# Attention's extra products at other steps, small products behind the scores, statistics ahead of the maximum

## The reference, cut to what matters

```python
def _L1_attn_ref(x, w_qkv, w_out, b_out):
    ...
    dots = jnp.einsum('bhid,bhjd->bhij', q, k) * SCALE
    m = jax.nn.softmax(dots, axis=-1)
    diag = jnp.diagonal(m, axis1=-2, axis2=-1)
    mu = diag.mean(axis=-1, keepdims=True)
    sd = diag.std(axis=-1, ddof=1, keepdims=True)
    keep = jnp.abs((diag - mu) / sd) <= Z_THRESH
    valid = keep[..., :, None] & keep[..., None, :]
    masked = jnp.where(valid, dots, NEG)
    attn = jax.nn.softmax(masked, axis=-1)
    ...
    out = jnp.einsum('bhij,bhjd->bhid', attn, v)
    out = out.transpose(0, 2, 1, 3).reshape(b, n, h * d)
    return out @ w_out.T + b_out
```

## Time and profile before

| | |
|---|---|
| median of 3 runs | 1979.87 us (1979.25 to 1979.98) |
| the profiled execution's own time | 1980.71 us |
| its span, first to last instruction | 1979.4 us |
| TensorE busy | 1786.4 us (90%) |
| VectorE, ScalarE, GpSimd busy | 1404.6, 1159.7, 1193.8 us |
| granted TensorE clock, mean | 0.987 |
| attention, first `scores` to last head's end | about 736 to 1850 us |

### The profile page before, as it was taken

How to read it: one execution, slowest core, us unless ns; L and a number is a source line. 1 busy time by engine, 2 the same in 40 slices (tenths; PEclk the granted TensorE clock), 3 DMA queues, 4 the chain that set the end, 5 groups by cost and what they waited for, 6 DMA issues and landing times. The chain is left out here.

```text
span 1979.4 us, 29905 instructions
## 1 busy us (share of the span) xinstructions
PE 1786.4 (90%) x11064; PEld 1213.2 (61%) x11064; DVE 1404.6 (71%) x2493; ACT 1159.7 (59%) x1715; POOL 1193.8 (60%) x660
## 2 busy tenths in 40 slices
PE   9998999789998986899989899898989898988888
PEld 5873444336875654666666667666666676665466
DVE  5617899986427754677777777777777777787676
ACT  5326777745326456666666666666666666663544
POOL 5542767963535430576666767676767666667454
PEclk9998999999999997999999999999999999999999
DMA  2000000000000013212122121212121212100100
GB/s 96 1 0 0 0 0 0 0 1 0 1 20 29 1 51 75 52 45 58 45 48 55 38 64 35 68 35 58 45 57 46 57 45 56 44 12 17 53 6 16
DMA packets 43665, 66.03 MB, mean 33 GB/s; under 512 B 24769, under 2 KB 26177, under 8 KB 43265
## 3 DMA queue, kind: packets, MB, share of 16 engines
q1 hardware_dynamic: 43056, 63.54, 12.4%
q10 hardware_dynamic: 432, 0.59, 0.1%
q0 software_dynamic: 32, 0.00, 0.0%
HBM read 29.05 MB, written 1.24 MB: 15 GB/s over the span
## 5 line engine op out<-in xcount | busy, mean ns | idle before, releaser
L2409 POOL TENSOR_TENSOR at_e_lo<-at_e,at_e_hi 128x1024 fp32r<-128x1024 f32 x256 | 613.1, 2395 | 353.9 <-DVE at_e_hi L2382 348.4
L2165 ACT ACTIVATE at_e<-at_ps,at_dropped 128x1024 f32<-128x1024 f32 x256 | 285.7, 1116 | 199.7 <-PE at_ps L1878 189.3
L2157 ACT ACTIVATE at_ps<-at_ps,at_neg_diag 128x1024 f32<-128x1024 f32 x256 | 278.6, 1089 | 138.3 <-DVE at_neg_diag L2253 137.0
L2262 DVE CUSTOM_DVE_ANT_0 at_ps<-at_ps,at_mask 128x1024 f32<-128x1024 f32 x256 | 314.1, 1227 | 3.0 <-PE at_ps L1998 1.3
L2382 DVE CAST at_e_hi<-at_e 128x1024 fp32r<-128x1024 f32 x256 | 247.8, 968 | 31.8 <-ACT at_e L2165 30.1
L1957 PE MATMUL at_ps<-at_kq,at_qk 64*128 64x512 f32 x768 | 235.3, 414 | 6.9 <-DVE at_row_max L2262 4.5
L1958 PE MATMUL at_ps<-at_qk,at_kq 64*128 64x512 f32 x768 | 235.7, 414 | 0.0
L2007 PE MATMUL at_ps<-at_qk,at_kq 64*128 64x512 f32 x768 | 224.4, 398 | 1.6 <-DVE at_row_max L2262 1.2
L2008 PE MATMUL at_ps<-at_kq,at_qk 64*128 64x512 f32 x768 | 224.6, 399 | 0.0
L1878 PE MATMUL at_pv_ps<-at_e_hi,at_v_hi 64*128 64x512 f32 x980 | 218.0, 436 | 0.0
L1056 POOL TENSOR_TENSOR mb_work<-mb_work,mb_c 128x1024 f32<-128x1024 f32 x64 | 151.6, 2370 | 97.7 <-DVE mb_work L1025 97.6
(11 more groups left out here) (392 smaller groups left out, 4243.1 us busy)
## 6 DMA issues: line engine op xcount, KB each, us to landing
at_kq<-at_qk SPq DMA_DIRECT2D x128, 256.0 KB, 4.2
at_mask<-at_mask_dram SPq DMA_DIRECT2D x32, 256.0 KB, 3.6
at_recips<-at_recip_row SPq DMA_DIRECT2D x31, 256.0 KB, 4.4
ffn_h_raw<-in_h SPq DMA_DIRECT2D x2, 1024.0 KB, 8.0
at_head_w_raw<-in_w_qkv SPq DMA_DIRECT2D x32, 64.0 KB, 3.9
x<-in_x SPq DMA_DIRECT2D x4, 256.0 KB, 5.0
moe_gate_in<-in_gate_in SPq DMA_DIRECT2D x2, 512.0 KB, 4.0
moe_up_in<-in_up_in SPq DMA_DIRECT2D x2, 512.0 KB, 4.3
```

The costliest lines, as they stand in the source:

```text
L2157: act.eng.activation(ps[:], ps[:], ACT.Exp, scale=SCALE, bias=m.small["neg_diag"][s][:, blk:blk + 1], accum_out=m.small["sums"][s][:, blk: ...
L2165: act.eng.activation(m.e[e % 2][:], slot("turned_scores", h, blk)[:], ACT.Exp, scale=SCALE, bias=m.small["dropped"][h % SLOTS][:, blk:blk ...
L2262: dve.eng.tensor_tensor_reduce(out=ps[:], in0=ps[:], in1=m.mask[h % 2][:], scale=1.0, scalar=-BIG, op0=ALU.add, op1=ALU.max, accum_out=m.s ...
L2409: pool.eng.tensor_tensor(m.e_lo[e % 3][:], m.e[e % 2][:], m.e_hi[e % 3][:].bitcast(F32), ALU.subtract).then_inc(sem["at_lo"])
```

## The change

All five queues of attention are affected:

- `AT_QK` goes from -8 to -3 and `AT_SPLIT` from -11 to -6: `qk` now falls on step 5, three steps ahead of the head's first `scores` (it was step 0, eight ahead); the split of weights falls on step 2 of GpSimd (it was 5); the rounding, the rest, the four DMAs and the next head's weight load follow at step 6 (they were at 1).
- `AT_OUT` goes from 39 to 43: `out` falls on step 3 (it was 7), its sum into x on step 4 (it was 0). The last pair keeps offset 39 (`AT_LAST_OUT`). The loop has one more step.
- TensorE issues `scores` ahead of the small products (it was behind them).
- VectorE's order in a step becomes: `rest_of_qk`, `rest_of_values`, the sum into x, `diagonal`, `first_stats`, `negate_mean`, `negate_square` with `keeps`, `mask_rows`, `shift_rows`, the denominators' reciprocal, the cast, `best`.

The offsets of turned scores (22) and weighing (24), `values`, and the offsets of the small products stay.

```diff
--- before.py
+++ after.py
@@ -1560,7 +1560,7 @@
 
 
 
-AT_FIRST, AT_LAST = -BLK * 2, BLK * (NH - 1) + BLK * 5 + 1
+AT_FIRST, AT_LAST = -BLK * 2, BLK * (NH - 1) + BLK * 5 + 2
 STATS, DEVS = 8, 5
 HI, LO = 0, 1
 TOP, LOW = slice(0, HD), slice(HD, P)
@@ -1569,8 +1569,8 @@
 PARTS = 4
 
 
-AT_SPLIT, AT_QK, AT_SCORES, AT_STATS, AT_MEAN, AT_SQUARE, AT_MASK, AT_BEST, AT_SHIFT = -11, -8, 0, 8, 9, 10, 11, 13, 21
-AT_TURNED, AT_PV, AT_PV_OUT, AT_RECIP, AT_SPREAD, AT_NORM, AT_OUT = 22, 24, 32, 34, 35, 37, 39
+AT_SPLIT, AT_QK, AT_SCORES, AT_STATS, AT_MEAN, AT_SQUARE, AT_MASK, AT_BEST, AT_SHIFT = -6, -3, 0, 8, 9, 10, 11, 13, 21
+AT_TURNED, AT_PV, AT_PV_OUT, AT_RECIP, AT_SPREAD, AT_NORM, AT_OUT, AT_LAST_OUT = 22, 24, 32, 34, 35, 37, 43, 39
 
 
 def due(t, offset, n=1):
@@ -1589,8 +1589,10 @@
 
 
 def pair_due(t):
+    if t == LAST * BLK + AT_LAST_OUT:
+        return LAST
     at = due(t, AT_OUT)
-    return at[0] if at and at[0] % 2 == 1 else None
+    return at[0] if at and at[0] % 2 == 1 and at[0] != LAST else None
 
 
 def small_due(t):
@@ -2089,6 +2091,8 @@
         apart = bool(weighed and tested)
         if at := due(t, AT_TURNED, BLK):
             turned_scores(*at)
+        if at := due(t, AT_SCORES, BLK):
+            scores(*at)
         if at := due(t, AT_MEAN):
             mean(at[0])
         if at := due(t, AT_SQUARE):
@@ -2097,8 +2101,6 @@
             turn_mask(at[0])
         if at := due(t, AT_SHIFT):
             turn_shift(at[0])
-        if at := due(t, AT_SCORES, BLK):
-            scores(*at)
         if apart:
             weigh(*weighed, False)
         if tested:
@@ -2336,13 +2338,6 @@
                 attention_later_norm_dve(c, m)
         if at := group_due(t - 1):
             rest_of_values(*at)
-        if (at := due(t, AT_RECIP)) and at[0] == LAST:
-            last_norm()
-        elif at:
-            dve.wait_ge(sem["den_move"], 16 * (at[0] + 1))
-            dve.eng.tensor_scalar(m.den[:], m.den[:], 1.0 / BIG, None, ALU.max).then_inc(sem["at_recip"])
-            dve.wait_ge(sem["at_recip"], 2 * at[0] + 1)
-            dve.eng.reciprocal(m.recip[:], m.den[:]).then_inc(sem["at_recip"])
         if (h := pair_due(t - 1)) is not None:
             pair, b = h % HEADS // 2, h // HEADS
             cols = slice(b * SEQ, (b + 1) * SEQ)
@@ -2362,18 +2357,26 @@
             else:
                 dve.wait_ge(sem["x_attn"], h // 2)
                 dve.eng.tensor_tensor(c.x[:, cols], c.x[:, cols], slot("out", h)[:], ALU.add).then_inc(sem["x_attn"])
+        if at := due(t, AT_SCORES, BLK):
+            diagonal(*at)
+        if at := due(t, AT_STATS):
+            first_stats(at[0])
         if at := due(t, AT_MEAN):
             negate_mean(at[0])
         if at := due(t, AT_SQUARE):
             negate_square(at[0])
+            keeps(at[0])
         if at := due(t, AT_MASK):
             mask_rows(at[0])
         if at := due(t, AT_SHIFT):
             shift_rows(at[0])
-        if at := due(t, AT_SCORES, BLK):
-            diagonal(*at)
-        if at := due(t, AT_STATS):
-            first_stats(at[0])
+        if (at := due(t, AT_RECIP)) and at[0] == LAST:
+            last_norm()
+        elif at:
+            dve.wait_ge(sem["den_move"], 16 * (at[0] + 1))
+            dve.eng.tensor_scalar(m.den[:], m.den[:], 1.0 / BIG, None, ALU.max).then_inc(sem["at_recip"])
+            dve.wait_ge(sem["at_recip"], 2 * at[0] + 1)
+            dve.eng.reciprocal(m.recip[:], m.den[:]).then_inc(sem["at_recip"])
         if at := due(t, AT_TURNED, BLK):
             e = at[0] * BLK + at[1]
             dve.wait_ge(sem["at_exp"], e + 1)
@@ -2382,8 +2385,6 @@
             dve.eng.tensor_copy(m.e_hi[e % 3][:], m.e[e % 2][:]).then_inc(sem["at_hi"])
         if at := due(t, AT_BEST, BLK):
             best(*at)
-        if at := due(t, AT_SQUARE):
-            keeps(at[0])
     dve.wait_ge(sem["x_attn"], ATTN_SUMS)
```

## The result

The changed kernel takes 1904.49 us (median of 4 runs, 1902.68 to 1906.3) where the kernel before, run beside it, took 1979.92 (4 runs, 1979.25 to 1980.74). The ratio is 0.9624, with a 95% interval of 0.9613 to 0.9636: 75 us faster. The forecast was 1926, so the direction is right and the gain is 21 us larger than the sum gave.

A forecast was written before the change was run, and what follows sets the result against it. TensorE's in-order queue and its waits bound the kernel: 33.59 us a head, 4.04 of it waits. Work of 29.55 plus 2.1 of new waits gives 31.65, saving 1.94 times 28, 54.3 us: 1926, range 1884 to 1962.

The forecast's parts named there:

- The mean's wait: TensorE at mean for rest_of_qk: the 1.7 us a head lost there goes, 0.35 stays at a best.
- The mask: TensorE at turn_mask: 1.35 us a head for at_dropped goes; 0.55 for the last best, 0.25 and 0.1 come.
- the lock: VectorE and GpSimd's exclusive port: the split of weights may hold up keeps, adding 0.25 us at turn_mask (0 to 0.7).
- The small products behind the scores: TensorE's best in steps 1, 2, 5 waits for VectorE's reading of them: 0.1 each, 0.3 us a head (0 to 0.6).
- the residual: What stays of steps taking 3.42 us instead of 3.33 on TensorE: 0.25 us a head.
- The parts' DMAs: A head's first scores wait for the four DMAs: nothing at the median, 1.2 us at worst, 0.2 taken.
- The extra products: TensorE's work beyond plain steps, per head: values 0.67 us, out 0.86, the latter the same before and after.
- The fill: The first heads' short steps at the start of attention: 2 us longer (-3 to +6).
- VectorE and GpSimd as the bound: Rival: their chain sets 32.8 us a head, giving 1957 us; chance 0.18.
- The waits vanish wholly: Rival: TensorE's cover is as long as the work hidden, 3.74 us a head saved, 1875 us; chance 0.13.
- The parts a step late: Rival: a head's first scores wait a step more, 34.95 us a head, 2018 us; chance 0.06.
- Nothing gained: Rival: the waits only change their names, 1980 us; chance 0.03.

The follow-up runs named there:

- s1: The kernel before with the offsets of qk and the split of weights alone changed (to -3 and -6): 1952.88 us, ratio 0.9855 to the kernel before.
- s2: The kernel before with scores ahead of the small products on TensorE, nothing else changed: 1956.11 us, ratio 0.9872 to the kernel before.
- u1: The changed kernel with qk and the split of weights back at their old offsets (-8 and -11): 1941.76 us, ratio 0.981 to the kernel before.
- s3: The kernel before with VectorE's new order alone, TensorE's queue as before: 1998.69 us, ratio 1.0091 to the kernel before.
- u4: The changed kernel with out back at step 7 (offset 39): 1900.67 us, ratio 0.9591 to the kernel before.
- v2: The changed kernel with out back at step 7 and the denominators' reciprocal at step 1 instead of 2: 1897.87 us, ratio 0.9578 to the kernel before.
- w3: The changed kernel with VectorE's whole order as before, TensorE's left as changed: 1929.95 us, ratio 0.9747 to the kernel before.
- w1: The changed kernel with qk and the split of weights one step earlier (offsets -4 and -7): 1938.58 us, ratio 0.9797 to the kernel before.
- u3: The changed kernel with keeps again at the end of VectorE's step 2: 1926.8 us, ratio 0.9725 to the kernel before.

## Why the prediction was right, and where it was off

*The mean's wait.* Predicted gone, and it is. What takes its place is the first `best` of step 6 for `rest_of_qk`: 0.26 a head from start to start, forecast 0.35. From the last `qk` pair to that `best` are 2.77 us (timeline of the kernel after), forecast 2.88:

```profile
1372.22 0.39 PE L1880 MATMUL at_ps<-at_xn_lo,at_head_w_hi 64*128 64x512 f32 x2
...
1372.65 1.03 ACT L2144 ACTIVATE at_qk<-at_ps 128x1024 fp32r<-128x1024 f32 x1 [1.63 <-PE at_ps L1880]
...
1373.71 1.22 DVE L2239 TENSOR_TENSOR at_qk<-at_ps,at_qk 128x1024 fp32r<-128x1024 f32 x1 [1.84 <-ACT at_qk L2144]
...
1374.99 0.50 PE L1999 MATMUL at_ps<-at_kq,at_qk 64*128 64x512 f32 x1
```

*The mask.* Mis-sized, the largest term: 0.55 + 0.25 + 0.1 = 0.9 forecast, 0.65 measured (0.46 in three heads of four, 1.23 where `values` precede). The first of these terms is also not what its own figures give: `best` at +4.45 and TensorE at +4.0 make 0.45. The 0.25 for the lock did not come. VectorE's chain of step 2 and GpSimd's (same kernel, timeline):

```profile
1359.67 0.31 DVE L2294 TENSOR_SCALAR at_keep<-at_dev,at_limit,at_varies 128x8 f32<-128x8 f32 x1
...
1360.01 0.17 DVE L2297 TENSOR_SCALAR at_dropped<-at_keep 128x8 f32<-128x8 f32 x1
1360.09 0.16 DVE L2377 TENSOR_SCALAR at_den<-at_den 128x8 f32<-128x8 f32 x1
...
1360.41 0.65 DVE L2385 CAST at_e_hi<-at_e 128x1024 fp32r<-128x1024 f32 x1
1360.97 1.23 DVE L2264 CUSTOM_DVE_ANT_0 at_ps<-at_ps,at_mask 128x1024 f32<-128x1024 f32 x1
```

```profile
1356.78 2.40 POOL L2410 TENSOR_TENSOR at_e_lo<-at_e,at_e_hi 128x1024 fp32r<-128x1024 f32 x1 [0.85 <-DVE at_e_hi L2385]
...
1359.49 0.46 POOL L1760 TENSOR_TENSOR at_head_w_lo<-at_head_w_raw,at_head_w_hi 128x128 fp32r<-128x128 f32 x1
```

at_e_lo ends at 1359.18. The third operation of `keeps` starts at 1359.67, beside the split, which is the case that the prediction feared. But only 0.28 us of the split are left then: it ends at 1359.95, the operation at 1359.98, after 0.31. The split takes 0.46 where the earlier trace rows had 0.82. From the scores' start at 1358.05 `best` ends at 1362.26 with the read of the maximum, +4.2, forecast +4.45.

*The small products behind the scores, and the residual.* Mis-sized: forecast 0.3 + 0.25, measured 0.29 together, 0.24 in steps 0 to 2 and 0.05 in step 5. The wait of a `best` for the small products' reader is in these 0.24.

*The parts' DMAs* with the `best` of step 7: forecast 0.2 + 0.1, measured 0.22, in 21 of 27 heads but by 0.9 at most. So the statement that no head waits at the median was wrong in its count, and the quoted estimate of 2.6 us for a landing, whose fit is of another issuing path than SyncE's, does not hold here: the last parts land 3.7, 4.3 and 5.8 us after their issue (min, median, max; kernel after).

*The extra products.* The price of `out` was 0.80 a head (forecast 0.86) and that of `values` 0.69 (0.67). But the price of `out` is not "the same before and after": in the kernel before step 7 took 5.43 with it and 3.29 without, so 2.14, against 1.65 in step 3 after. In s1, where only `qk` and the split moved, it is 1.43 in step 7.

*The sum.* 26.64 + 1.38 + 0.69 + 0.80 + mask 0.65 + small and rest 0.29 + `best` 0.26 + parts 0.22 = 30.93, measured 30.90, forecast 31.65. Of the 0.75 between, 0.25 are the mask, 0.26 the small products and the rest, 0.09 the `best`, 0.08 the parts, 0.04 the extra products, 0.03 rounding. Times 28 it is 21 us, the whole miss. Every wait was put too high, so the errors add up: 30.90 lies just under the 31 to 32.4 that the prediction named for eight steps. The fill (+0.9, forecast +2) and the rest (+0.6, forecast -2) nearly cancel.

*What the prediction did not see.* The shift row's DMA: hidden before by the small products' place, and uncovered as soon as `turn_shift` moves behind the scores (s2, u1) or VectorE makes the row behind `diagonal` (s3, u1). The change hides it again only because `qk` went to step 5. That is why `qk` was worth 37 us and not the 17 expected of u1. It cost the forecast nothing, which was luck: the shift's DMA was put down "as before", which came out right without the reason having been seen. And `out` in step 3 was counted as neutral; u4 shows it is worse by 0.2 to 0.33% of the time.

*The rivals.* VectorE and GpSimd as the bound: not so; with 623.5 and 620.9 us busy of 865.2, 242 and 244 us are to spare. That is a little more than before for VectorE (237) and less for GpSimd (299), but TensorE's waits that are left are named above and none is for at_e_lo. The waits vanish wholly (29.85 a head): no; 1.4 us a head stay, and the ring places show which. The parts a step late: no, 0.9 at most. Nothing gained: no; VectorE's order alone even lost 18 us.

*What stays open.* Why v2 got 0.18 a head of the 0.36 (at_den 0.16, the reciprocal 0.20) that leaving the reciprocals out of the chain should give. What the extra 3 us of w3's fill are. The start of attention differs by up to 3 us between profiles of kernels that are the same up to there, so differences of this size in a span are not told apart.

## What to carry to other kernels

On an in-order queue, price an extra product by where its reader stands in the ring of result buffers, and look at every place three behind the one you move it to: one step's difference (w1) cost 34 us, with 0.94 us a head at that place and 0.40 at the uncovered DMA. Before moving a product away, or another behind it, list the DMAs that it covers; in five of these kernels the shift row's DMA became the new wait. And test parts of such a change together, since here they sum to 36 us singly and 74 jointly, with one of them a loss on its own.

## What the runs showed of the hardware that was not expected

VectorE operations that waited for GpSimd cost much less when they run in its gaps, or beside a short operation that is nearly done. On the same work, the denominators' first went from 1.34 us in one step 2 of before to 0.16: before it began while at_e_lo ran in 30 of 31 heads, now in one. The third operation of `keeps` went from a median of 1033 ns to 293 and is still beside GpSimd: before it began during at_e_lo in 30 of 32 heads and ended about 0.03 us after it, now it begins during the split in nearly all and ends about 0.03 us after that. Its own 0.29 us hide the 0.26 that the split has left; in one head, where 0.38 were left, it took 405 ns. The cast's mean in step 7 went from 2.21 us to 0.85, while it grew from 0.69 to 1.07 in step 3 and from 0.82 to 1.12 in step 6; over the stretch it was 932 ns and is now the first of these groups (times, busy us, mean ns; kernel after):

```profile
L2385 DVE CAST at_e_hi<-at_e 128x1024 fp32r<-128x1024 f32 x216 | 175.9, 814 | 10.4 <-ACT at_e L2167 7.7 <-issue 0.3
L2422 POOL TENSOR_TENSOR at_heads_out<-at_pv_sb,at_recips 64x1024 f32<-64x1024 f32 x27 | 64.6, 2392 | 3.6
L1760 POOL TENSOR_TENSOR at_head_w_lo<-at_head_w_raw,at_head_w_hi 128x128 fp32r<-128x128 f32 x27 | 12.4, 461 | 2.2
```

GpSimd gains too: the normalization takes 2392 ns where the earlier trace rows had 2855, the split 461 where it had 825. The three VectorE groups make 216 x 0.118 + 27 x (0.72 + 1.18) = 77 of VectorE's 80 us less. How much of it was on TensorE's path is not shown; in w3 the denominators' operation takes 1.45 us in the median and a head takes no longer than in u3, where it takes 0.20. So busy time of these two engines is no measure of their work: the same instructions took 11% less of VectorE in another order.

Not every small operation waits: the one on 128x1 elements ahead of that of `keeps` took 153 to 154 ns in all 32 heads after and 147 to 152 before, though before it began while at_e_lo was running in 30 of them. The Trainium skill (SBUF — State Buffer, "SBUF: two separate sides") gives the exclusive lock only to some kinds of VectorE operation, those in a two-port mode or with two inputs from SBUF. The rows agree that there are two kinds, and that the 128x8 operation of 0.3 us is of the kind that waits.
